# A record sort on one core: the rank picked out by TensorE and ScalarE in place of a product on VectorE, and three stages issued one unit further ahead

## The chip, the core and the metric

The kernel runs on one core of a Trainium2 chip. The metric is the time of one execution on the device in microseconds; lower is better. It is measured over several runs, and one more execution was profiled. The engines are named TensorE (PE, weight loads PEld), VectorE (DVE), ScalarE (ACT), GpSimd (POOL) and SyncE (SP). Each runs its own list of instructions in order and waits on semaphores for the others.

## The reference

Four layers of a graph network over 6250 nodes with 128 features and 200000 edges; each layer's result is added to its input and normalised. Only the edges matter here: every layer sums messages over the edges of a node.

```python
agg = jax.ops.segment_sum(msg, dst, num_segments=n_nodes)          # layer 0, mean over relations' messages
agg = jax.ops.segment_sum(val_exp[:, :, None] * h_neigh[edge_col], edge_row, num_segments=n)   # layer 1, attention
msg = jnp.where((edge_types == 0)[:, None], m_data, m_ctrl)        # layer 2
agg = jax.ops.segment_sum(msg, dst, num_segments=X.shape[0])
messages = norm[:, None] * h[col]                                  # layer 3
x = _layernorm(x + layer(x, edges))                                # four times
```

`src` and `dst` are data, so the kernel first sorts the edges on the chip into blocks by the tile of their target and the tile of their source. The four layers then work on those blocks.

## The kernel before, in words

About the first quarter of the span is the sort; the layers behind it need its whole result. An edge is a record of small bf16 fields, and 128 partitions times 1568 columns hold all of them. The sort has three levels, each of which distributes records by one digit of at most 14 values. The work is cut into **226 units**: 49 of level 1 (32 columns of records each, 14 digit values: tiles 448 wide), and then, in an order of groups of seven, 91 of level 2 and 86 of level 3 (28 columns each: tiles 392 wide). Forty-nine units of level 3 have a further place for records that overflow a bucket (`u.extra`; 16 digit places, tiles 448 wide), and seven units of level 2 are 112 wide. The units form two phases, level 1 and the rest, and the second begins when the last unit of the first is evicted.

A unit n passes through these steps, in lists written out by hand for each engine:

1. ScalarE, `double`: the unit's fields are copied in pairs into `V`, a ring of three (L429, L433, L437).
2. VectorE, `hot`: `O`, a one-hot of each record's digit, from `V` (L677).
3. TensorE, `count`: `pR` receives, for every record and every digit value, the number of records with this digit in front of it. One matmul with a triangle over the partitions (`tri_b`, L574) and 7 or 13 with ones (`ones_b`, L577) add into one PSUM bank of two.
4. ScalarE, `looked`: `R`, a bf16 copy of `pR` (L446).
5. VectorE: `M` = `O` times `R` (L730), which keeps only the count at the record's own digit; then `ranks`, a sum over the digits: `rank` (L687). A unit with an extra bucket adds three small instructions that change `O` and `rank` (L697, L699, L700).
6. ScalarE, `paired`: `place`, the rank in pairs (L455).
7. VectorE: `VO`, the fields times the one-hot (L740), and `PM`, a one-hot of the place in 128 columns (L91).
8. TensorE, `route`: 28 or 32 matmuls of `PM` and `VO` into `pV` (L593). ScalarE, `evict`: into `terms`, `second` or `recs` (L464, L470, L483).

VectorE's list for unit n is M(n), hot(n+1), ranks(n), VO(n), PM(n). TensorE's is count(n+1), route(n). ScalarE's is paired(n), evict(n-1), looked(n+1), in 147 units a copy for a small projection that TensorE makes in between (`xT` L539, `B` L544), then double(n+2), and in some units larger copies. In twelve units VectorE also unpacks sorted words (`words`, L712 and L714) between VO and PM.

The functions the diff touches:

Of the kernel before, what the change touches and what calls it, by code (L numbers as in the profile page):

```python
# [33 lines left out]
DIG, DIG_SHIFT, DIG_RECIP = 14, 16, 4682  # L34
# [4 lines left out]
def gnn_four_layers_kernel(nc, t, out):  # L39
# [30 lines left out]
    with ExitStack() as ctx:  # L70
        def sb(name, shape, dt, c=ctx):
            return c.enter_context(nc.sbuf_tensor(name, shape, dt))
# [84 lines left out]
        with ExitStack() as c1:  # L157
# [11 lines left out]
            zero_b = sb("zero_b", [P, P], BF16, c1)  # L169
# [4 lines left out]
            O = sb("O", [P, 2, 512], BF16, c1)  # L174
            R = sb("R", [P, 2, 512], BF16, c1)
            M = sb("M", [P, 512], BF16, c1)
# [25 lines left out]
                     "s_dup", "s_hot", "s_cnt", "s_look", "s_mul", "s_rank", "s_more", "s_pair", "s_val", "s_perm", "s_out", "s_ev",  # L202
                     "s_tp0", "s_xt0", "s_y0", "s_own0", "s_high0", "s_rest0", "s_mid0", "s_low0", "s_wt0", "s_total", "s_words", "s_named", "s_kind", "s_left", "s_last")
            (loads, pads, consts, tri_made, prep, fields, blanks, packed, s_pad, s_load, s_xin, s_stored, turned, wt_made,
             s_dup, s_hot, s_cnt, s_look, s_mul, s_rank, s_more, s_pair, s_val, s_perm, s_out, s_ev,
# [26 lines left out]
            done_with = {u.d: n + 1 for n, u in enumerate(units) if u.level == 3}  # L232
            SPLIT_AT, LIN_AT = A_N + 2, A_N + 28
            assert LIN_AT + 3 * NT <= UN
            PREP, FIELDS, PACKED = 15, 9, 6
            PADDED = 96

# [55 lines left out]
            with nc.Block() as block:  # L293
# [33 lines left out]
                def _(gp):  # L327
# [13 lines left out]
                    gp.memset(zero_b[:, :], 0.0).then_inc(consts, 1)  # L341
# [26 lines left out]
                    gp.wait_ge(consts, 11)  # L368
# [22 lines left out]
                def _(act):  # L391
# [47 lines left out]
                    def looked(n):  # L439

                        u = units[n]
                        k = u.npos * u.ngrp * u.w
                        act.wait_ge(s_cnt, n + 1)
                        if n >= 2:
                            act.wait_ge(s_mul, n - 1)
                        act.activation(R[:, n % 2, 0:k], pR[n % 2][:, 0:k], ACT.Copy).then_inc(s_look, 1)  # L446

                    def paired(n):

                        u = units[n]  # L450
                        cols = u.npos * u.ngrp
                        act.wait_ge(s_rank, n + 1)
# [71 lines left out]
                    for a, b in phases:  # L524
                        double(a)
                        double(a + 1)
                        looked(a)
                        for n in range(a, b):
                            paired(n)
                            if n > a:  # L530
                                evict(n - 1)
                            if n + 1 < b:
                                looked(n + 1)
                            i, sub = slot_of(n)
                            if sub == 1:
                                act.wait_ge(s_tp, i + 1)
                                if i >= 1:
                                    act.wait_ge(s_y, i)
                                act.activation(xT[:, :], pL[:, 0, :], ACT.Copy).then_inc(s_xt, 1)  # L539
                            if sub == 2:  # L540
                                act.wait_ge(s_y, i + 1)
                                if i % G7 == 0:
                                    act.wait_ge(s_rest, i // G7 + 1)
                                act.activation(B[:, i, :], pL[:, 1, :], ACT.Copy).then_inc(s_own, 1)  # L544
                            if n + 2 < b:
                                double(n + 2)
                            if n == A_N - 8:
                                weights_turned()
                            m, when = divmod(n - SPLIT_AT, 2)
                            if 1 <= m <= NB and when == 0:  # L550
                                mid_part(m - 1)
                            if 0 <= m < NB and when == 0:
                                high_part(m)
                            for d in range(LATE):
                                if n == done_with[d] + 3:
                                    places_and_high(d)
                                if n == done_with[d] + 6:
                                    sources_and_middle(d)
                        evict(b - 1)
# [4 lines left out]
                def _(pe):  # L564

                    def count(n):

                        u = units[n]
                        row = u.ngrp * u.w
                        k = u.npos * row  # L570
                        pe.wait_ge(s_hot, n + 1)
                        if n >= 2:
                            pe.wait_ge(s_look, n - 1)
                        pe.matmul(pR[n % 2][:, 0:k], tri_b[:, :], O[:, n % 2, 0:k], start=True, stop=False, skip_group_check=True)  # L574
                        for j in range(u.npos - 1):
                            m = u.npos - 1 - j
                            mm = pe.matmul(pR[n % 2][:, (j + 1) * row:k].rearrange("p (m r) -> p m r", r=row), ones_b[:, :],  # L577
                                           O[:, n % 2, j * row:(j + 1) * row].unsqueeze(1).broadcast_to([P, m, row]), start=False, stop=m == 1, skip_group_check=True)
                        mm.then_inc(s_cnt, 1)
# [17 lines left out]
                    pe.wait_ge(consts, 11)  # L597
# [32 lines left out]
                def _(v):  # L630
# [36 lines left out]
                    v.wait_ge(consts, 11)  # L667

                    def hot(n):

                        u = units[n]
                        cols = u.npos * u.ngrp
                        v.wait_ge(s_dup, n + 1)
                        if n >= 2:
                            v.wait_ge(s_val, n - 1)
                        o = O[:, n % 2, 0:cols * u.w].rearrange("p (n a b) -> p n a b", b=2, a=u.w // 2)
                        v.tensor_tensor(o, iota_1[:, 0:u.w].rearrange("p (a b) -> p a b", b=2).unsqueeze(1).broadcast_to([P, cols, u.w // 2, 2]),  # L677
                                        fields_of(n)[:, u.nf, :, :].unsqueeze(2).broadcast_to([P, cols, u.w // 2, 2]), ALU.is_equal).then_inc(s_hot, 1)

                    def ranks(n):  # L680
# [3 lines left out]
                        v.wait_ge(s_mul, n + 1)  # L684
                        if n >= 2:
                            v.wait_ge(s_pair, n - 1)
                        ins = v.tensor_reduce(rank[:, n % 2, 0:cols], M[:, 0:cols * u.w].rearrange("p (n a) -> p n a", a=u.w), AX.X, ALU.add)  # L687
                        if u.extra is None:
                            ins.then_inc(s_rank, 1)
                            return  # L690
                        ins.then_inc(s_more, 1)
                        mores[0] += 2
                        g, b = u.extra[1:]
                        o = O[:, n % 2, 0:cols * u.w].rearrange("p (a g w) -> p a g w", g=2, w=u.w)[:, :, g, :]
                        r = rank[:, n % 2, 0:cols].rearrange("p (a g) -> p a g", g=2)[:, :, g]
                        v.wait_ge(s_more, mores[0] - 1)
                        v.scalar_tensor_tensor(out=o[:, :, DIG], in0=r, scalar=float(P), in1=o[:, :, b], op0=ALU.is_ge, op1=ALU.mult).then_inc(s_more, 1)  # L697
                        v.wait_ge(s_more, mores[0])
                        v.scalar_tensor_tensor(out=r, in0=o[:, :, DIG], scalar=-float(P), in1=r, op0=ALU.mult, op1=ALU.add).then_inc(s_rank, 1)  # L699
                        v.tensor_tensor(o[:, :, b], o[:, :, b], o[:, :, DIG], ALU.subtract).then_inc(s_more, 1)  # L700
                        mores[0] += 1
# [19 lines left out]
                    mores = [0]  # L721
                    for a, b in phases:
                        hot(a)
                        for n in range(a, b):
                            u = units[n]
                            cols = u.npos * u.ngrp
                            v.wait_ge(s_look, n + 1)
                            if n >= 1:
                                v.wait_ge(s_rank, n)
                            v.tensor_tensor(M[:, 0:cols * u.w], O[:, n % 2, 0:cols * u.w], R[:, n % 2, 0:cols * u.w], ALU.mult).then_inc(s_mul, 1)  # L730
                            if n + 1 < b:
                                hot(n + 1)
                            ranks(n)
                            if n >= 2:
                                v.wait_ge(s_out, n - 1)
                            if u.extra is not None:
                                v.wait_ge(s_more, mores[0])
                            pairs = fields_of(n)[:, 0:u.nf, :, :]
                            where = O[:, n % 2, 0:cols * u.w].rearrange("p (n a b) -> p n a b", b=2, a=u.w // 2)
# [1743 lines left out]
```

## Time and profile before

| | us |
|---|---|
| median of 3 runs (lowest, highest) | 4307.43 (4306.51, 4310.26) |
| profiled execution, its own time | 4305.91 |
| its span, from the first to the last instruction | 4304.2 |
| VectorE busy in the span | 3648.7 (85%) |
| TensorE busy in the span | 3657.9 (85%) |
| ScalarE busy in the span | 2047.2 (48%) |
| GpSimd busy in the span | 431.4 (10%) |
| mean granted TensorE clock, as a share of 2.4 GHz | 0.945 |

The shares are means over all stages of the program, so they say little about the sort, which is the only stage that the diff touches. What bounds it is read from its own stretch, from the first O at 60.19 us to the last words at about 1135 us.

### The profile page before, as it was taken

To read this page: it belongs to the slowest core of one execution; us is meant where nothing else is said; L and a number is where in the kernel's file an instruction comes from. 1 tells how busy PE (TensorE), PEld (TensorE's weight loads), DVE (VectorE), ACT (ScalarE), POOL (GpSimd) and SP (SyncE) were. 2 spreads that over 40 slices of the span, in tenths; PEclk is the share of its full clock that TensorE was granted. 3 is DMA by queue.
4 is the path that set the end of the run, shared out by engine and by line. 5 is a ranking of instruction groups with operands and counts; after the bars stand their busy time and mean duration, and the time that the engine had idled before them with its cause. 6 is when DMAs were issued, how large, how long until landed. Compare 5 with 4: busy or idle time off the path is not lost. (4 is left out here: it accounts for less than half of the span.)

```text
span 4304.2 us, 94469 instructions
## 1 busy us (share of the span) xinstructions
PE 3657.9 (85%) x38991; PEld 3057.2 (71%) x38992; DVE 3648.7 (85%) x4714; ACT 2047.2 (48%) x4002; POOL 431.4 (10%) x335
## 2 busy tenths in 40 slices
PE   2665666666599999968999999997999999989998
PEld 2554555555466666648999999996888888867776
DVE  7999999999877777768999999998666666778897
ACT  2333333333355555532333333333666666757776
POOL 3002221230111111110000000001000000000000
PEclk9778899998799999978999999998999999989999
DMA  3000000000032222210000000001333333300000
GB/s 103 1 1 1 2 2 1 2 2 2 31 117 108 108 108 108 108 58 2 2 2 2 2 2 2 2 2 39 101 103 102 101 100 101 97 1 10 5 10 10
DMA packets 104807, 178.63 MB, mean 42 GB/s; under 512 B 11690, under 2 KB 101559, under 8 KB 104244
## 3 DMA queue, kind: packets, MB, share of 16 engines
q1 hardware_dynamic: 103892, 170.07, 12.1%
q8 instruction: 317, 5.19, 0.5%
q10 hardware_dynamic: 480, 2.40, 0.2%
q14 instruction: 118, 0.97, 0.1%
HBM read 86.93 MB, written 85.49 MB: 40 GB/s over the span
## 5 line engine op out<-in xcount | busy, mean ns | idle before, releaser
L97 DVE TENSOR_TENSOR both_hot<-iota_own,recs 128x1792 bf16<-128x1792 bf16 (+1 forms) x686 | 756.5, 1106 | 252.4 <-PE rR L1437 143.1
L1801 ACT ACTIVATE gC<-qC 128x896 f32<-128x896 f32 x343 | 314.6, 917 | 647.3 <-PE qC L1821 647.3
L1833 PE MATMUL qO<-A,gC 128*128 128x132 f32 x4802 | 615.2, 280 | 0.0
L593 PE MATMUL pV<-VO,PM 128*128 128x70 bf16 (+4 forms) x6524 | 295.3, 210 | 326.1 <-issue 322.7
L1833 PEld LDWEIGHTS qO<-A,gC 128*128 128x128 f32 x4802 | 566.4, 190 | 0.0
L593 PEld LDWEIGHTS pV<-VO,PM 128*128 128x128 bf16 x6524 | 272.3, 107 | 350.2 <-issue 348.8
L1445 PE MATMUL rO<-sl_f,terms 128*128 128x512 bf16 (+1 forms) x2058 | 500.1, 354 | 4.1 <-ACT sl_f L1403 2.5
L91 DVE TENSOR_TENSOR PM<-iota_b,place 128x3584 bf16<-128x3584 bf16 (+1 forms) x226 | 480.5, 2126 | 0.8 <-ACT place L455 0.8
L2145 ACT ACTIVATE some_r<-rC 128x512 fp32r<-128x512 f32 (+1 forms) x686 | 336.1, 543 | 253.0 <-PE rC L2175 252.6
L1403 ACT ACTIVATE sl_f<-rC 128x896 bf16<-128x896 f32 x343 | 314.0, 916 | 279.9 <-PE rC L1425 279.7
L91 DVE TENSOR_TENSOR places_hot<-iota_own,recs 128x896 bf16<-128x896 bf16 x700 | 403.2, 620 | 51.8 <-PE tC L2414 21.4
L1437 PE MATMUL rR<-rel_hot,both_hot 128*128 128x65 bf16 x2450 | 409.1, 193 | 0.0
L2396 ACT ACTIVATE tables_r<-tC 128x896 fp32r<-128x896 f32 x350 | 321.0, 919 | 143.5 <-PE tC L2414 142.8
L2426 PE MATMUL tO<-tables_r,Xr 128*128 128x448 f32 x1400 | 371.4, 387 | 9.1 <-ACT tables_r L2396 4.8
L1639 DVE TENSOR_TENSOR g<-sl_f 128x2688 bf16<-128x2688 bf16 (+1 forms) x229 | 363.5, 1587 | 0.2 <-PE qC L1821 0.2
L2187 PE MATMUL rK<-some_r,Xr 128*128 128x512 f32 (+1 forms) x1372 | 363.1, 386 | 0.0
L1821 PE MATMUL qC<-g,sl_f 128*128 128x128 bf16 x4908 | 313.5, 220 | 48.8 <-DVE g L1639 48.6
L2187 PE MATMUL rA<-all_r,Xr 128*128 128x512 f32 (+1 forms) x1372 | 342.1, 371 | 1.9 <-DVE all_r L1946 1.9
L1821 PEld LDWEIGHTS qC<-g,sl_f 128*128 128x128 bf16 x4908 | 292.1, 98 | 58.0 <-DVE g L1639 54.5
L577 PE MATMUL pR<-O,ones_b 128*128 128x392 bf16 (+16 forms) x2644 | 326.5, 281 | 0.0
L1445 PEld LDWEIGHTS rO<-sl_f,terms 128*128 128x128 bf16 x2058 | 201.0, 98 | 174.8 <-ACT sl_f L1403 5.9
L577 PEld LDWEIGHTS pR<-O,ones_b 128*128 128x128 bf16 x2644 | 255.7, 110 | 94.2 <-issue 30.2
(296 smaller groups left out, 6083.9 us busy)
## 6 DMA issues: line engine op xcount, KB each, us to landing
tables<-sl_f SPq DMA_DIRECT2D x343, 224.0 KB, 1.9
sl_f<-tables SPq DMA_DIRECT2D x343, 224.0 KB, 2.5
edges<-terms SPq DMA_DIRECT2D x1, 3528.0 KB, 11.2
B<-in_x SPq DMA_DIRECT2D x1, 2744.0 KB
out<-B SPq DMA_DIRECT2D x7, 392.0 KB
terms<-in_edge_type ACTq DMA_DIRECT2D x2, 686.0 KB
terms<-in_edge_weight ACTq DMA_DIRECT2D x1, 686.0 KB
recs<-in_src SPq DMA_DIRECT2D x1, 686.0 KB
```

Source lines behind the costliest of these rows:

```text
L91: return v.tensor_tensor(o.rearrange("p n (a b) -> p n a b", b=2), (iota_own if own else iota_b)[:, at:at + w].rearrange("p (a b) -> p a b ...
L97: return v.tensor_tensor(o.rearrange("p n k (a b) -> p (n k) a b", b=2), iota_own[:, 0:w].rearrange("p (a b) -> p a b", b=2).unsqueeze(1). ...
L577: mm = pe.matmul(pR[n % 2][:, (j + 1) * row:k].rearrange("p (m r) -> p m r", r=row), ones_b[:, :], O[:, n % 2, j * row:(j + 1) * row].unsq ...
L593: mm = pe.matmul(pV[n % 2][:, g * row:(g + 1) * row].rearrange("p (f b) -> p f b", f=u.nf), PM[:, n % 2, col, :], values[:, :, col, :], st ...
L1437: return pe.matmul(pR[:, to:to + DW], both_hot[:, U % 3, j, 0, :], rel_hot[:, K % 2, a % FOUR * n + j, 0:DW], start=a == 0 and j == 0, sto ...
L1445: mm = pe.matmul(pO[:, h, 0:(hi - lo) * P], X[:, a, s, :], of_half(kept[U % RING], h), start=a == 0 and s == 0, stop=a == NT - 1 and s == ...
L1639: v.tensor_tensor(h1[:, U % 2, 0:n, :, :].rearrange("p n s (a b) -> p n s a b", b=2), bare[U % 3][:, 0:n, 1, :].rearrange("p n (a b) -> p ...
L1821: mm = pe.matmul(pC[U % 2][:, tile_in_group(q, j), :], bare[U % 3][:, j, 0, :], h1[:, U % 2, j, s, :], start=s == 0 and (q > 0 or j != 1), ...
L1833: mm = pe.matmul(pO[i % SUMS][:, 0:XW], Cs[:, U % 2, j, :], A[:, a, :], start=a == 0, stop=a == NT - 1)
L2145: act.activation(of_half(some_r[:, U % 2, :], h).rearrange("p (n d) -> p n d", d=P), pC[Q % 3][:, 0:hi - lo, :], ACT.Copy).then_inc(s_cs, 1)
L2187: mm = pe.matmul((pA if whole else pK)[:, h, 0:(hi - lo) * P], Xr[:, a, s * P:(s + 1) * P], of_half((all_r if whole else some_r)[:, U % 2, ...
L2426: mm = pe.matmul(pO[:, h, 0:HW], Xr[:, max(b - 1, 0), s * P:(s + 1) * P], table_h[:, h, :], start=b == 0 and s == 0, stop=b == NX - 1 and ...
```

## The change

The product M on VectorE goes. A constant `lift` (2048 on the diagonal) is made on GpSimd at the start, and a further matmul with it in `count` adds 2048 to `pR` at each record's own digit. ScalarE's eviction becomes a Relu with a bias of -2048 per partition (`drop`), so that it writes `M` itself: the count at the own digit, zero elsewhere. `R` is gone; `M` has two buffers, `O` three. The one-hot, the counts and the evictions are issued two units ahead where they were one, and the doubled fields three ahead where they were two. A semaphore `s_taken` (rank read) takes the place of `s_mul` and `s_rank`.

```diff
-            zero_b = sb("zero_b", [P, P], BF16, c1)
+            lift = sb("lift", [P, P], BF16, c1)
+            drop = sb("drop", [P, 1], F32, c1)
...
-            O = sb("O", [P, 2, 512], BF16, c1)
-            R = sb("R", [P, 2, 512], BF16, c1)
-            M = sb("M", [P, 512], BF16, c1)
+            O = sb("O", [P, 3, 512], BF16, c1)
+            M = sb("M", [P, 2, 512], BF16, c1)
...
+                    gp.tensor_scalar(lift[:, :], ident_f[:, :], LIFT, None, ALU.mult).then_inc(consts, 1)
-                    gp.wait_ge(consts, 11)
+                    gp.wait_ge(consts, 12)
...
-                            act.wait_ge(s_mul, n - 1)
-                        act.activation(R[:, n % 2, 0:k], pR[n % 2][:, 0:k], ACT.Copy).then_inc(s_look, 1)
+                            act.wait_ge(s_taken, n - 1)
+                        act.activation(M[:, n % 2, 0:k], pR[n % 2][:, 0:k], ACT.Relu, bias=drop[:, 0:1]).then_inc(s_look, 1)
...
                         double(a)
                         double(a + 1)
+                        double(a + 2)
                         looked(a)
+                        looked(a + 1)
                         for n in range(a, b):
                             paired(n)
                             if n > a:
                                 evict(n - 1)
-                            if n + 1 < b:
-                                looked(n + 1)
...
-                                double(n + 2)
+                                looked(n + 2)
...
+                        pe.matmul(pR[n % 2][:, 0:k], lift[:, :], O[:, n % 3, 0:k], start=False, stop=False, skip_group_check=True)
...
                         count(a)
+                        count(a + 1)
                         for n in range(a, b):
-                            if n + 1 < b:
-                                count(n + 1)
+                            if n + 2 < b:
+                                count(n + 2)
...
                         hot(a)
+                        hot(a + 1)
                         for n in range(a, b):
...
-                            v.wait_ge(s_look, n + 1)
-                            if n >= 1:
-                                v.wait_ge(s_rank, n)
-                            v.tensor_tensor(M[:, 0:cols * u.w], O[:, n % 2, 0:cols * u.w], R[:, n % 2, 0:cols * u.w], ALU.mult).then_inc(s_mul, 1)
-                            if n + 1 < b:
-                                hot(n + 1)
                             ranks(n)
+                            if n + 2 < b:
+                                hot(n + 2)
```

(`double(n + 3)` stands just ahead of `looked(n + 2)`, behind the copies of the projection.)

VectorE's list in a unit with an extra bucket, level 3, before:

```order
L730 TENSOR_TENSOR M<-O,R 128x448
L677 TENSOR_TENSOR O<-iota,V 128x392
L687 TENSOR_REDUCE rank<-M 128x28
L697 SCALAR_TENSOR_TENSOR O<-rank,O 128x14
L699 SCALAR_TENSOR_TENSOR rank<-O,rank 128x14
L700 TENSOR_TENSOR O<-O 128x14
L740 TENSOR_TENSOR VO<-O,V 128x1792
L91 TENSOR_TENSOR PM<-iota_b,place 128x3584
```

The same place on VectorE in the changed program:

```order
L698 TENSOR_REDUCE rank<-M 128x28
L705 SCALAR_TENSOR_TENSOR O<-rank,O 128x14
L707 SCALAR_TENSOR_TENSOR rank<-O,rank 128x14
L708 TENSOR_TENSOR O<-O 128x14
L688 TENSOR_TENSOR O<-iota,V 128x448
L743 TENSOR_TENSOR VO<-O,V 128x1792
L91 TENSOR_TENSOR PM<-iota_b,place 128x3584
```

M is gone, and the one-hot O, now of the unit after next, stands between the last of the small instructions and VO.

ScalarE's list around one copy of the projection (xT), before; M and R are of the unit whose counts are ready, place is of the unit in work:

```order
L483 ACTIVATE recs<-pV 128x14x4 x2
L483 ACTIVATE recs<-pV 128x4
L446 ACTIVATE R<-pR 128x448
L539 ACTIVATE xT<-pL 128x128
L437 ACTIVATE V<-second 128x280
L455 ACTIVATE place<-rank 128x56
```

The same place on ScalarE in the changed program:

```order
L490 ACTIVATE recs<-pV 128x14x4 x2
L490 ACTIVATE recs<-pV 128x4
L546 ACTIVATE xT<-pL 128x128
L437 ACTIVATE V<-terms 128x336
L450 ACTIVATE M<-pR,drop 128x392
L462 ACTIVATE place<-rank 128x56
```

The eviction of the counts moved behind xT and V, so it is now the last thing ahead of the next unit's place.

## Rows read from the trace of the kernel before

**Rows 1.** Stretches: us; busy (instructions) of PE, PEld, DVE, ACT, POOL; clock; DMA.

```profile
66.00:304.00 238.00, 150.28 (x1953) 121.75 (x1954) 232.84 (x241) 82.40 (x197) 0.00 (x0) 0.80 0.07 19
304.00:312.00 8.00, 5.68 (x53) 4.54 (x52) 6.12 (x9) 1.87 (x5) 0.00 (x0) 0.50 0.00 1
312.00:1130.00 818.00, 537.84 (x7695) 436.37 (x7693) 782.79 (x1080) 302.36 (x1116) 179.29 (x113) 0.88 0.01 2
```

**Rows 2.** Waits of VectorE in the sort: us in total, times, longest us.

```profile
DVE M L730 <- ACT R L446: 28.3, 34, 3.3
DVE O L677 <- ACT V L433: 4.8, 8, 3.6
DVE PM L91 <- ACT place L455: 0.8, 1, 0.8
```

**Rows 3.** Timeline, level 1, VectorE: start us, duration us, instruction.

```profile
106.68 0.38 DVE L730 TENSOR_TENSOR M<-O,R 128x448 bf16<-128x448 bf16 x1
106.98 0.38 DVE L677 TENSOR_TENSOR O<-iota,V 128x448 bf16<-128x448 bf16 x1
```

**Rows 4.** Timeline, a plain unit of level 3, VectorE.

```profile
606.95 2.02 DVE L91 TENSOR_TENSOR PM<-iota_b,place 128x3584 bf16<-128x3584 bf16 x1
608.89 0.35 DVE L730 TENSOR_TENSOR M<-O,R 128x392 bf16<-128x392 bf16 x1
609.16 0.35 DVE L677 TENSOR_TENSOR O<-iota,V 128x392 bf16<-128x392 bf16 x1
609.43 0.55 DVE L687 TENSOR_REDUCE rank<-M 128x28 f32<-128x392 bf16 x1
609.90 0.96 DVE L740 TENSOR_TENSOR VO<-O,V 128x1568 bf16<-128x1568 bf16 x1
610.79 2.02 DVE L91 TENSOR_TENSOR PM<-iota_b,place 128x3584 bf16<-128x3584 bf16 x1
```

**Rows 5.** Timeline, end of a unit with an extra bucket, VectorE.

```profile
605.54 0.17 DVE L699 SCALAR_TENSOR_TENSOR rank<-O,rank 128x14 f32<-128x14 bf16 x1
605.63 0.21 DVE L700 TENSOR_TENSOR O<-O 128x14 bf16<-128x14 bf16 x1
605.95 1.09 DVE L740 TENSOR_TENSOR VO<-O,V 128x1792 bf16<-128x1792 bf16 x1
```

**Rows 6.** Groups: busy us, mean ns of one; idle before, releaser.

```profile
L730 DVE TENSOR_TENSOR M<-O,R 128x448 bf16<-128x448 bf16 (+2 forms) x226 | 87.0, 385 | 28.3 <-ACT R L446 28.3
L446 ACT ACTIVATE R<-pR 128x448 bf16<-128x448 f32 (+2 forms) x226 | 115.2, 510 | 220.9 <-PE pR L577 220.4
L455 ACT ACTIVATE place<-rank 128x56 bf16<-128x56 f32 (+1 forms) x226 | 57.8, 256 | 408.7 <-DVE rank L687 313.9 <-DVE rank L699 94.6
L355 POOL TENSOR_SCALAR terms<-terms 128x1568 int32<-128x1568 int32 x1 | 4.8, 4777 | 0.1
```

**Rows 7.** Timeline, TensorE, one route and one count at two times.

```profile
310.20 1.79 PE L593 MATMUL pV<-VO,PM 128*128 128x70 bf16 x28 [0.91 <-issue]
311.80 0.52 PE L574 MATMUL pR<-O,tri_b 128*128 128x392 bf16 x1
312.12 2.33 PE L577 MATMUL pR<-O,ones_b 128*128 128x364 bf16 x13
...
609.07 1.38 PE L593 MATMUL pV<-VO,PM 128*128 128x64 bf16 x28 [2.69 <-issue]
614.62 0.93 PE L593 MATMUL pV<-VO,PM 128*128 128x56 bf16 x28
615.39 0.33 PE L574 MATMUL pR<-O,tri_b 128*128 128x392 bf16 x1
615.55 1.27 PE L577 MATMUL pR<-O,ones_b 128*128 128x364 bf16 x13
```

**Rows 8.** Timeline, VectorE, the starts of both phases.

```profile
63.18 0.39 DVE L730 TENSOR_TENSOR M<-O,R 128x448 bf16<-128x448 bf16 x1 [2.60 <-ACT R L446]
...
305.82 0.36 DVE L730 TENSOR_TENSOR M<-O,R 128x392 bf16<-128x392 bf16 x1 [3.26 <-ACT R L446]
```

More of the change, by code:

```diff
@@ L232, in gnn_four_layers_kernel @@
             done_with = {u.d: n + 1 for n, u in enumerate(units) if u.level == 3}
+            mores_of = {n: 3 * i for i, n in enumerate(n for n, u in enumerate(units) if u.extra is not None)}
             SPLIT_AT, LIN_AT = A_N + 2, A_N + 28
@@ L236, in gnn_four_layers_kernel @@
             PADDED = 96
+            LIFT = 2048.0
+            assert 8 * P < LIFT and DIG * P < LIFT
             LATE = ND1 - 2
@@ L340, in _ @@
                     gp.memset(ones_b[:, :], 1.0).then_inc(consts, 1)
-                    gp.memset(zero_b[:, :], 0.0).then_inc(consts, 1)
+                    gp.memset(drop[:, :], -LIFT).then_inc(consts, 1)
                     gp.memset(ident_f[:, :], 0.0).then_inc(tri_made, 1)
@@ L451, in paired @@
                         cols = u.npos * u.ngrp
-                        act.wait_ge(s_rank, n + 1)
+                        if u.extra is None:
+                            act.wait_ge(s_taken, n + 1)
+                        else:
+                            act.wait_ge(s_more, mores_of[n] + 2)
                         if n >= 2:
@@ L544, in _ @@
                                 act.activation(B[:, i, :], pL[:, 1, :], ACT.Copy).then_inc(s_own, 1)
+                            if n + 3 < b:
+                                double(n + 3)
                             if n + 2 < b:
-                                double(n + 2)
+                                looked(n + 2)
                             if n == A_N - 8:
@@ L573, in count @@
                             pe.wait_ge(s_look, n - 1)
-                        pe.matmul(pR[n % 2][:, 0:k], tri_b[:, :], O[:, n % 2, 0:k], start=True, stop=False, skip_group_check=True)
+                        pe.matmul(pR[n % 2][:, 0:k], tri_b[:, :], O[:, n % 3, 0:k], start=True, stop=False, skip_group_check=True)
+                        pe.matmul(pR[n % 2][:, 0:k], lift[:, :], O[:, n % 3, 0:k], start=False, stop=False, skip_group_check=True)
                         for j in range(u.npos - 1):
@@ L577, in count @@
                             mm = pe.matmul(pR[n % 2][:, (j + 1) * row:k].rearrange("p (m r) -> p m r", r=row), ones_b[:, :],
-                                           O[:, n % 2, j * row:(j + 1) * row].unsqueeze(1).broadcast_to([P, m, row]), start=False, stop=m == 1, skip_group_check=True)
+                                           O[:, n % 3, j * row:(j + 1) * row].unsqueeze(1).broadcast_to([P, m, row]), start=False, stop=m == 1, skip_group_check=True)
                         mm.then_inc(s_cnt, 1)
@@ L666, in _ @@
                     v.wait_ge(prep, PREP)
-                    v.wait_ge(consts, 11)
+                    v.wait_ge(consts, 12)
                     def hot(n):
@@ L736, in _ @@
                             if u.extra is not None:
-                                v.wait_ge(s_more, mores[0])
+                                v.wait_ge(s_more, mores_of[n] + 3)
                             pairs = fields_of(n)[:, 0:u.nf, :, :]
-                            where = O[:, n % 2, 0:cols * u.w].rearrange("p (n a b) -> p n a b", b=2, a=u.w // 2)
+                            where = O[:, n % 3, 0:cols * u.w].rearrange("p (n a b) -> p n a b", b=2, a=u.w // 2)
                             v.tensor_tensor(VO[:, n % 2, 0:cols * u.nf * u.w].rearrange("p (f n a b) -> p f n a b", b=2, a=u.w // 2, f=u.nf),
```

29 lines of the change are left out of this document (12 added, 17 removed).

## The prediction

> **What bounds the kernel now.** The busy shares of the whole span say nothing here, because the diff touches only the sort; so I read the stretches of the sort first. In level 1 VectorE is busy 232.84 of 238.00 us and in levels 2 and 3 782.79 of 818.00, that is 98% and 96%, while TensorE has 150.28 and 537.84 and ScalarE 82.40 and 302.36 [rows 1]. The reader is to see that VectorE has hardly a gap and every other engine many. The list of waits then tells what VectorE's gaps are: 28.3 us in 34 waits of the product M for the evicted counts R, and 4.8 us in 8 waits of the one-hot O for V [rows 2]. It hardly ever waits for `place` (0.8 us, once). Everything behind the sort needs its whole result, so a microsecond taken out of VectorE's list is a microsecond of the kernel, as long as the others keep up.
>
> **What goes: 226 products.** A neighbour starts before an instruction has ended, so the price of one is from its start to the next start, not its duration. A 448-wide M starts at 106.68 and the next O at 106.98: 0.30 us of a duration of 0.38 [rows 3]. A 392-wide one takes 608.89 to 609.16: 0.27 [rows 4]. By the loops there are 98 of 448 (49 of level 1, 49 with an extra bucket), 121 of 392 and 7 of 112, for which I take half of 0.27. That is 98 x 0.30 + 121 x 0.27 + 7 x 0.13 = **63.0 us**. The instruction behind PM is then the reduction, which waits for a look that was due a unit earlier.
>
> The Trainium skill ("VectorE: DVE Perf Modes", The DRAIN you can't avoid) says that the next operation does not start until the pipe is empty. By that, a product would give back its whole busy time, 87.0 us in the group of M [rows 6], 24 more than I count. The starts 0.30 us apart under a duration of 0.38 [rows 3] speak against it.
>
> **What goes: waits for the counts.** Two of the 34 waits are the starts of the phases, 2.60 and 3.26 us [rows 8], where nothing can lie ahead. The other 32 are 28.3 - 2.60 - 3.26 = **22.4 us**. They come where TensorE is slow: R(n+1) is behind route(n-1) and count(n+1), both of which start only after PM(n-1), and M(n+1) wants it one VectorE unit later. In the change the counts that come behind the same route are those of the unit after, wanted a whole unit later. Of the waits of O for V, the one at the phase start (3.6, the longest [rows 2]) stays; the other seven, 1.2 us, go, since V too is a unit ahead: **1 us**.
>
> **What goes: a bubble in 49 units.** In a unit with an extra bucket VO must wait for the last small write: from its start at 605.63 to VO at 605.95 it is 0.32 us, where the one ahead of it, which nobody waits for, takes 605.54 to 605.63, 0.09 [rows 5]. In the change the one-hot stands between, which reads nothing of it. I take 0.20 us of the 0.23: **10 us**, bounds 0 and 11.
>
> **What comes.** *TensorE:* one matmul of 392 or 448 columns per unit. The triangle of the same width takes 615.39 to 615.55, 0.16 us, at the high clock and 311.80 to 312.12, 0.32 us, at the low one [rows 7]. TensorE's work in a plain unit at the high clock becomes route 0.93 (to its modelled end) + count 615.39 to 616.82, 1.43, + 0.16 = 2.5 us against a VectorE unit of 608.89 to 610.79 plus the PM of 1.94 (606.95 to 608.89), less M: 1.90 + 1.94 - 0.27 = 3.57 us [rows 4, 7]. Hidden by 1 us; the projection (three matmuls and a transpose in turn over three units) fits into it.
>
> *ScalarE:* the same evictions, 0.51 us on average [rows 6], now with a bias read per partition; it is idle most of the sort, so only two of them, at the phase starts, are on the path. The Trainium skill ("ScalarE: Activation LUTs", What ACT_TABLE_LOAD costs) gives about 0.09 us for each such operand; by it two evictions on the path would cost 0.2 us, and no row here shows it apart. Relu is no table switch: both built programs have four table loads.
>
> *The cover that could go* is the order on ScalarE: `place` of unit n+1 now stands behind the eviction of the counts of unit n+2. Count from the start of unit n's reduction, which is the end of PM(n-1). PM(n+1) wants `place` after a whole unit, 3.57, and reduction, O and VO of the next, 0.47 + 0.27 + 0.89 = 1.63: at 5.2 us. ScalarE's chain at the high clock is route 0.93, count 1.59, eviction 0.5 + 0.1 (a guess for the bias), place 0.26 [rows 6], and some 0.2 for handing over: 3.6 us, 1.6 early. At the low clock it is route 1.79, count 311.80 to 314.45, 2.65, + 0.32, then 0.6, 0.26, 0.2: 5.8 us, 0.6 late [rows 4, 7]. So a unit at the low clock can still cost 0.6 us, and if it does not, nothing is lost. The stretch of levels 2 and 3 had a granted clock of 0.88, which is 24% of it at 1.2 GHz, and the slow route at 609.07 came after 2.69 us of idle TensorE [rows 1, 7]. Shorter VectorE units and one more matmul shorten that idle time; long gaps stay in the twelve units with `words` and at the phase starts. I take **3 us** (some five stalls of 0.6); bounds 0 and 32 x 0.6 = 19.
>
> *Start of the sort:* GpSimd makes `lift` as the last constant, and VectorE and TensorE wait for it. The nearest row is a tensor_scalar of 1568 columns in 4.78 us [rows 6]; for 128 that is 0.4, with a fixed part 0.5. The longer first count (0.4) and the missing M and O on the chain cancel: **0.5 us**.
>
> *Start of the second phase*, at the low clock (0.50 in that stretch [rows 1]): ScalarE now evicts the second unit's counts ahead of the first `place`, and a slow count of 2.97 us with an eviction of 0.6 lies there where reduction, O and VO fill only 1.63: 1.9 late, less the one-hot that is already done, 0.27, and a little for the longer VO of level 2: **1.5 us**, bounds 0.3 and 3.
>
> **Sum.** 63.0 + 22.4 + 1 + 10 - 3 - 0.5 - 1.5 = 91.4 us off the profiled execution's 4305.9 (span 4304.2 and 1.7 around it): 4214.5. The median of the runs shown lies 1.5 above that execution, so I say **4216 us**.
>
> **Rivals.**
> *The waits come back as waits for `place`.* For it: the chain above is late by 0.6 in a slow unit, and the 32 old waits averaged 0.7 us. Against it: TensorE has less idle time, and 1.6 us of slack at the high clock. Then the 22.4 us are not gained: 4216 + 22 - 3 = 4235; 0.18.
> *TensorE becomes the bound and the kernel slower.* If the granted clock stayed at 1.2 GHz, a unit would take TensorE 1.79 + 2.65 + 0.32 = 4.8 us and the projection some 0.5 more per unit, 5.3 against VectorE's 4.2 on average with its words and small instructions ((818 - 81) / 177). Each slow unit then costs 1.1 us; 91 us are eaten at 83 slow units in a row of 177, about half; with all of them slow it is +195 - 91, 4410. Against it: 24% were slow when TensorE had more idle time [rows 1]. 0.04.
> *The product is worth its whole busy time.* 87.0 instead of 63.0: 4192; 0.03. The skill's page quoted above is its reason, the starts in rows 3 and 4 are against it.
> *The change does not do what it says*, because VectorE meets the same length of chain elsewhere: waits for `place` of 0.4 us in each of 226 units would take all of it, and the slack of 1.6 us must be wrong by 2. 0.03, time 4307.
>
> **Numbers.** My forecast (4207 to 4226) has 0.72. With the returning waits in part or whole, to 4240, it is 0.72 + 0.15; the lower end is the sum with no stalls and the full bubble, about 4210, less some microseconds for the phases behind the sort: 4205. Range **4205 to 4240**. What a measurement of this kernel can tell from no change is about 0.2%, 8.6 us. Faster: 0.72 + 0.18 + 0.03 = 0.93; same 0.03; slower 0.04.
>
> **What would show it.** Right: VectorE's list has four large instructions per unit, 3.57 us in plain units and 0.30 less than before in level 1; the waits of a reduction for the look are two, at the phase starts; the sort ends about 91 us earlier and every stage behind it is as long as before; the granted clock in the sort rises. The bubble is right if O follows the last small instruction within 0.15 us. Wrong: waits of PM for `place` of more than 10 us, a granted clock under 0.88 in levels 2 and 3, reductions that wait for M in mid-phase, or routes that start later than PM's end in many units.

## The result and the profile after

| | before | changed |
|---|---|---|
| median | 4308.85 us (4 runs, 4306.51 to 4313.77) | 4203.91 us (4 runs, 4203.23 to 4205.06) |
| profiled execution, its span | 4305.9, 4304.2 us | 4203.2, 4201.5 us |
| granted clock over the span | 0.945 | 0.958 |

The ratio is 0.9765 (95% interval 0.9754 to 0.9777; the quotient of the two medians is 0.9756): 104.9 us less by the medians, 102.7 between the profiled executions. The forecast was 4216, 91.4 less; the time lies 1.1 us under the low end of its range. The direction was right, the mechanism too, and one term was too small.

First the page of the changed kernel, its first lines:

```profile
span 4201.5 us, 94346 instructions
...
PE 3645.2 (87%) x39093; PEld 3045.7 (72%) x39218; DVE 3569.6 (85%) x4488; ACT 2086.5 (50%) x4002; POOL 451.9 (11%) x336
```

Next, stretches: us; busy (instructions) of PE, PEld, DVE, ACT, POOL; granted clock; DMA share, GB/s. They are cut at the first one-hot of level 1, at that of level 2, where VectorE's last `words` start, and at the end. Of the kernel before, by the same cut (other than that of [rows 1]):

```profile
60.19:302.20 242.01, 152.60 (x1963) 123.08 (x1963) 235.69 (x245) 83.03 (x199) 0.00 (x0) 0.80 0.10 28
302.20:1134.40 832.20, 546.36 (x7779) 443.00 (x7779) 791.73 (x1091) 305.05 (x1124) 179.29 (x113) 0.87 0.01 2
1134.40:4304.20 3169.80, 2958.98 (x29249) 2491.10 (x29249) 2583.05 (x3331) 1643.17 (x2668) 214.67 (x195) 0.97 0.16 52
```

And of the changed kernel:

```profile
60.17:287.17 227.00, 154.03 (x2012) 120.33 (x2012) 220.67 (x197) 87.92 (x198) 0.00 (x0) 0.84 0.10 29
287.17:1025.80 738.63, 537.71 (x7956) 431.86 (x7956) 724.82 (x914) 338.95 (x1124) 196.48 (x113) 0.93 0.01 2
1025.80:4201.50 3175.70, 2953.50 (x29125) 2493.52 (x29249) 2584.61 (x3331) 1643.20 (x2668) 215.57 (x195) 0.97 0.16 52
```

Level 1 is 15.0 us shorter, levels 2 and 3 are 93.6 shorter, and what follows is 5.9 longer: 15.0 + 93.6 - 5.9 = 102.7. The forecast had 14.7 in level 1 (49 products of 0.30), a loss of 0.5 ahead of the first one-hot, 91.4 - 14.7 + 0.5 = 77.2 in levels 2 and 3, and none behind. So 16.4 us are to be explained in levels 2 and 3, and 5.9 behind the sort. Below, "the sort" is the first two stretches, 1074.2 and 965.6 us.

The timeline of VectorE in level 1, changed kernel (start, duration, instruction):

```profile
189.63 0.61 DVE L698 TENSOR_REDUCE rank<-M 128x32 f32<-128x448 bf16 x1
190.16 0.37 DVE L688 TENSOR_TENSOR O<-iota,V 128x448 bf16<-128x448 bf16 x1
190.46 1.54 DVE L743 TENSOR_TENSOR VO<-O,V 128x2688 bf16<-128x2688 bf16 x1
191.92 2.28 DVE L91 TENSOR_TENSOR PM<-iota_b,place 128x4096 bf16<-128x4096 bf16 x1
194.13 0.60 DVE L698 TENSOR_REDUCE rank<-M 128x32 f32<-128x448 bf16 x1
```

Four instructions per unit, 194.13 - 189.63 = 4.50 us. Before it was 4.80, the product's 0.30 more: behind the product at 106.68 in [rows 3] the next one starts at

```profile
111.48 0.38 DVE L730 TENSOR_TENSOR M<-O,R 128x448 bf16<-128x448 bf16 x1
```

The end of a unit with an extra bucket, which answers to [rows 5]:

```profile
597.27 0.18 DVE L707 SCALAR_TENSOR_TENSOR rank<-O,rank 128x14 f32<-128x14 bf16 x1
597.36 0.21 DVE L708 TENSOR_TENSOR O<-O 128x14 bf16<-128x14 bf16 x1
597.45 0.39 DVE L688 TENSOR_TENSOR O<-iota,V 128x448 bf16<-128x448 bf16 x1
597.75 1.08 DVE L743 TENSOR_TENSOR VO<-O,V 128x1792 bf16<-128x1792 bf16 x1
```

The last small write is now followed after 0.09 us instead of 0.32, and VO follows the one-hot after its usual 0.30. The waits of VectorE in the sort (us in total, times, longest), answering to [rows 2]:

```profile
DVE rank L698 <- ACT M L450: 6.1, 2, 3.3
DVE PM L91 <- ACT place L462: 4.6, 8, 0.9
DVE O L688 <- ACT V L437: 3.6, 1, 3.6
```

Where 34 waits for counts stood, two are left, the phase starts; the rest of the old waits has not come back as waits for `place`. Of the groups (busy us, mean ns; idle before), two:

```profile
L450 ACT ACTIVATE M<-pR,drop 128x448 bf16<-128x448 f32 (+2 forms) x226 | 135.0, 597 | 111.1 <-PE pR L587 109.1 <-DVE rank L698 1.9
L584 PE MATMUL pR<-O,lift 128*128 128x448 bf16 (+2 forms) x226 | 85.6, 379 | 0.0
```

The eviction costs 597 ns against 510 [rows 6], and the new matmul stands in line with no idle time before it.

### The profile page after: what moved, and what is told of

Its sections match the earlier page's. It is cut to its first block and busy times, and to the rows that moved or that the text cites. A ratio compares the mean times of both kernels' runs of the same rounds, so it can differ in the third digit from the quotient of the medians.

```text
span 4201.5 us, 94346 instructions
## 1 busy us (share of the span) xinstructions
PE 3645.2 (87%) x39093; PEld 3045.7 (72%) x39218; DVE 3569.6 (85%) x4488; ACT 2086.5 (50%) x4002; POOL 451.9 (11%) x336
## 5 line engine op out<-in xcount | busy, mean ns | idle before, releaser
L603 PE MATMUL pV<-VO,PM 128*128 128x70 bf16 (+4 forms) x6524 | 268.4, 202 | 248.4 <-issue 242.4
L1448 PE MATMUL rO<-sl_f,terms 128*128 128x384 bf16 (+1 forms) x1934 | 471.2, 352 | 3.3 <-ACT sl_f L1406 2.5
L603 PEld LDWEIGHTS pV<-VO,PM 128*128 128x128 bf16 x6524 | 246.0, 102 | 274.2 <-issue 273.7
L587 PEld LDWEIGHTS pR<-O,ones_b 128*128 128x128 bf16 x2644 | 242.7, 105 | 98.9 <-issue 24.5
L587 PE MATMUL pR<-O,ones_b 128*128 128x392 bf16 (+16 forms) x2644 | 299.7, 267 | 0.0
```

The source lines that it names most:

```text
L603: mm = pe.matmul(pV[n % 2][:, g * row:(g + 1) * row].rearrange("p (f b) -> p f b", f=u.nf), PM[:, n % 2, col, :], values[:, :, col, :], st ...
L1448: mm = pe.matmul(pO[:, h, 0:(hi - lo) * P], X[:, a, s, :], of_half(kept[U % RING], h), start=a == 0 and s == 0, stop=a == NT - 1 and s == ...
```

## The experiments

Every row of this table is one kernel's profiled execution: stretches cut as above, and the median of its runs (of e3 and e4 one run each). The ratio is to runs of the kernel before taken beside it, whose medians are 4308.85 for the changed kernel and 4305.66 to 4306.65 for the others.

| kernel | level 1 | levels 2, 3 | sort | median (ratio to before, 95%) |
|---|---|---|---|---|
| before | 242.0 | 832.2 | 1074.2 | 4308.85 |
| changed | 227.0 | 738.6 | 965.6 | 4203.91 (0.9754 to 0.9777) |
| e1 look-ahead alone | 241.5 | 804.9 | 1046.4 | 4281.77 (0.9926 to 0.9959) |
| e2 lift alone | 233.7 | 766.9 | 1000.6 | 4241.83 (0.9829 to 0.9862) |
| e3 before, GpSimd's sort work cut | 241.9 | 802.9 | 1044.8 | 4300.41 |
| e4 changed, GpSimd's sort work cut | 227.0 | 709.3 | 936.2 | 4194.01 |
| e5 changed, one-hot behind VO | 227.0 | 767.0 | 994.0 | 4229.42 (0.9802 to 0.9832) |
| e6 changed, lift matmul twice | 227.4 | 742.2 | 969.6 | 4209.67 (0.9765 to 0.9795) |
| e7 changed, x copies ahead of the fields | 227.0 | 738.6 | 965.6 | 4201.29 (0.9742 to 0.9769) |
| e8 before, counts evicted behind V | 241.8 | 831.3 | 1073.1 | 4305.22 (0.9987 to 1.0005) |
| e9 changed, once more | 227.0 | 738.9 | 965.9 | 4205.32 (0.9745 to 0.9775) |

**e1: the look-ahead without the lift.** The kernel before with a third buffer of O and one-hots, counts and fields a unit further ahead; the product and R stay.

```diff
-            O = sb("O", [P, 2, 512], BF16, c1)
+            O = sb("O", [P, 3, 512], BF16, c1)
...
+                            if n + 3 < b:
+                                double(n + 3)
                             if n + 2 < b:
-                                double(n + 2)
+                                looked(n + 2)
...
-                            if n + 1 < b:
-                                count(n + 1)
+                            if n + 2 < b:
+                                count(n + 2)
...
-                            if n + 1 < b:
-                                hot(n + 1)
+                            if n + 2 < b:
+                                hot(n + 2)
                             ranks(n)
```

> The kernel before with the look-ahead alone: the product M stays on VectorE, the one-hots, counts, evictions and fields go one unit further ahead. My theory: the 22.4 us of waits for R in mid-phase and the 1.2 us of O for V go, the bubble in the 49 units with an extra bucket stays, and VectorE instructions lengthened by GpSimd fall by at most 10 us: 4274 to 4286 us. Rival (the chain of route, count and eviction comes back as waits for place): 4300 to 4309 us.

Measured 4281.77, in the expected range, sort 27.8 us shorter, nearly all of it (27.3) in levels 2 and 3. VectorE's waits from level 2 on:

```profile
DVE O L680 <- ACT V L433: 4.5, 3, 3.6
DVE PM L91 <- ACT place L455: 3.8, 5, 1.5
DVE M L734 <- ACT R L446: 2.9, 1, 2.9
```

The waits for counts are gone but for the phase start, and 3.8 us of waits for `place` have come. That the look-ahead removes these waits is shown. It gives 27.3 us net, and the forecast's terms for it come to 22.4 + 1 - 3 - 1.5 = 18.9.

**e2: the lift without the look-ahead.** The changed kernel with the order of before.

```diff
-                            if n + 3 < b:
-                                double(n + 3)
                             if n + 2 < b:
-                                looked(n + 2)
+                                double(n + 2)
...
-                            if n + 2 < b:
-                                count(n + 2)
+                            if n + 1 < b:
+                                count(n + 1)
...
                             ranks(n)
-                            if n + 2 < b:
-                                hot(n + 2)
+                            if n + 1 < b:
+                                hot(n + 1)
```

> The changed kernel with the look-ahead of the kernel before: the product is gone, one-hots, counts and evictions are one unit ahead, fields two. My theory: 63 us of products and 11 us of bubbles go, but the reduction now wants the evicted counts 0.3 us earlier than the product did, at the low clock about 1.9 us late, so the waits of VectorE for the eviction rise from 28 us to between 35 and 75: 4235 to 4275 us. Rival (the look-ahead buys nothing once the product is gone): 4200 to 4215 us.

Measured 4241.83, in the expected range, sort 73.6 us shorter. The waits for counts are now the reduction's (whole sort):

```profile
DVE rank L695 <- ACT M L450: 31.7, 37, 3.8
```

They had been expected to rise to between 35 and 75 us; they stayed near the 28.3 of before.

In levels 2 and 3 the two parts give 27.3 and 65.2 us, 92.5 together, of 93.6 measured for both: they add. In level 1 they do not: 0.5 + 8.4 of 15.0. Without look-ahead a level-1 unit that has lost its product is short enough to wait for its counts, which the unit of before was not: 24 of the 37 waits, 24.5 us, lie in levels 2 and 3, and the other 13, 7.3 us, in level 1, where the changed kernel has one, at the phase start.

**e3 and e4: is it GpSimd?** My first theory for the missing microseconds was that GpSimd's work in the sort stretches VectorE's instructions, less so in the changed order. Both kernels had GpSimd's elementwise steps cut to four columns.

```diff
-                        gp.tensor_tensor(xrest[:, :, :], B[:, T, :], X[:, T, 0, :], ALU.subtract).then_inc(s_rest, 1)
+                        gp.tensor_tensor(xrest[:, 0:1, 0:4], B[:, T, 0:4], X[:, T, 0, 0:4], ALU.subtract).then_inc(s_rest, 1)
```

(and the same for the other steps of the weights, the kinds and the low parts of x). What is left out VectorE clears behind the sort, where the two kernels take 3194.7 and 3196.2 us, so their medians say nothing of the sort; the stretches do.

> The kernel before with GpSimd's work inside the sort cut to four columns per instruction, which leaves out the low parts of x, the relation codes and the weights' rests (VectorE clears their places after the sort). My theory: the 35 us by which VectorE's starts in levels 2 and 3 are late beyond the waits named in the trace are GpSimd's doing, so the stretch from the first O to the last words falls from 1074 to about 1040 us. Rival (they are not GpSimd's): it stays above 1065 us.

> The changed kernel with the same cut of GpSimd's work in the sort. My theory: the same lateness is 20 us here, so the stretch from the first O to the last words falls from 966 to about 946 us, and the gap between the two kernels' stretches shrinks from 109 to about 94 us, which is near the forecast of 91. Rival (the missing 15 us have nothing to do with GpSimd): the gap stays at 105 to 111 us.

Levels 2 and 3 of the two kernels, columns as above:

```profile
301.13:1104.00 802.87, 540.42 (x7779) 438.74 (x7779) 758.47 (x1091) 305.38 (x1124) 81.40 (x69) 0.88 0.01 2
...
286.83:996.10 709.27, 521.74 (x7956) 422.22 (x7956) 696.72 (x913) 341.63 (x1124) 90.16 (x69) 0.96 0.01 2
```

As a reason for the missing microseconds the theory fell, though e3 came near its 1040 us. GpSimd's busy time falls from 179.29 to 81.40 us and from 196.48 to 90.16, and both sorts get 29.4 us shorter, so the gap between them stays 108.5. GpSimd costs VectorE much, but the same in both.

With GpSimd nearly out of the way the rest can be counted. I took each start-to-start distance of two neighbouring instructions of VectorE in levels 2 and 3, less the median for that pair, and call the sum the lateness (the starts of the phases left out). In e3 it is 27.9 us of M behind R (the list shows 28.4 - 3.3 = 25.1 of idle), **8.2 us of O behind V**, and 0.8 of PM behind `place`, 36.9 in all; in e4 it is 3.9, all for `place`. That is 33 us where the forecast had 18.9. (On the kernel before itself, where GpSimd's steps blur the count, M is late by 25.2.) The 8.2 is what I had missed: the list names 12 waits of O for V, 5.6 us, of which 3.6 is the phase start, so 2.0 of the 8.2. Most of the rest is in 30 one-hots that start late, 0.17 us on average, with no wait named: about half of that is idle time of under 0.15 us, which the list leaves out, and the end of the instruction ahead covers the other half. On the kernel before, one such place:

```profile
603.29 0.54 ACT L446 ACTIVATE R<-pR 128x448 bf16<-128x448 f32 x1 [1.94 <-PE pR L577]
603.73 0.27 ACT L544 ACTIVATE B<-pL 128x128 f32<-128x128 f32 x1
603.87 0.39 DVE L730 TENSOR_TENSOR M<-O,R 128x448 bf16<-128x448 bf16 x1 [0.83 <-ACT R L446]
603.89 0.44 ACT L437 ACTIVATE V<-second 128x280 bf16<-128x280 bf16 x1
604.36 0.36 DVE L677 TENSOR_TENSOR O<-iota,V 128x392 bf16<-128x392 bf16 x1
```

M waits for R. V stands behind R and a copy on ScalarE and ends at 604.33; O starts at 604.36, 0.49 after M instead of 0.30, and its row names no wait.

**e8: is O's lateness a cost of its own?** If V's place behind R were all, evicting the counts behind V would give it back on the kernel before.

```diff
                             if n > a:
                                 evict(n - 1)
-                            if n + 1 < b:
-                                looked(n + 1)
...
                             if n + 2 < b:
                                 double(n + 2)
+                            if n + 1 < b:
+                                looked(n + 1)
```

> The kernel before with one move on ScalarE: the eviction of the counts goes behind the projection's copies and the doubled fields, so V no longer stands behind R. The two runs without GpSimd's work put the 15 us that the forecast missed on VectorE's starts that were late without a wait named: O came 0.1 to 0.2 us late behind V in some 40 units, 8 us in all, where the list of waits showed 1.2. My new theory: this lateness of O goes, the late M stay, 4296 to 4302 us, the stretch from the first O to the last words 6 to 10 us shorter than 1074. Rival (O is late for another reason, or R comes later by as much): 4303 to 4309 us, the stretch above 1071.

Measured 4305.22, a ratio of 0.9987 to 1.0005: no change. Waits of VectorE in the sort:

```profile
DVE M L730 <- ACT R L446: 34.0, 42, 3.3
...
DVE O L677 <- ACT V L433: 3.6, 1, 3.6
```

O's waits are gone but for the phase start, and M's rose from 28.3 to 34.0: R is later by what V is earlier. The rival held. R and V, behind the count, are one chain on ScalarE, and a move within it gains nothing; the 23.4 us that I put down were the part of its cost that the list shows. Look-ahead takes VectorE off the chain (e1). It is not the only thing that helps: in e2, with the product gone and the look-ahead of before, the waits of O for V in mid-phase are down to one of 0.2 us.

**e5: the one-hot behind VO.** The changed kernel with O(n+2) moved, to see the bubble by itself.

```diff
                             ranks(n)
-                            if n + 2 < b:
-                                hot(n + 2)
...
                                             pairs.unsqueeze(3).broadcast_to([P, u.nf, cols, u.w // 2, 2]), ALU.mult).then_inc(s_val, 1)
+                            if n + 2 < b:
+                                hot(n + 2)
```

> The changed kernel with the one-hot of unit n+2 behind VO(n) where it stood between the small instructions and VO(n). My theory: VO again waits for the last small write in the 49 units with an extra bucket, 0.23 us each, 11 us more: 4213 to 4218 us. Rival (the gap before VO has another reason, or the place of the one-hot does not matter): 4202 to 4207 us.

Measured 4229.42, sort 28.4 us longer than the changed kernel's. One unit with an extra bucket, and the first row of the list of waits:

```profile
605.97 0.21 DVE L708 TENSOR_TENSOR O<-O 128x14 bf16<-128x14 bf16 x1
606.29 1.09 DVE L741 TENSOR_TENSOR VO<-O,V 128x1792 bf16<-128x1792 bf16 x1
607.30 0.86 DVE L688 TENSOR_TENSOR O<-iota,V 128x392 bf16<-128x392 bf16 x1
608.08 2.01 DVE L91 TENSOR_TENSOR PM<-iota_b,place 128x3584 bf16<-128x3584 bf16 x1
...
DVE PM L91 <- ACT place L462: 22.5, 26, 3.2
```

The bubble is back (605.97 to 606.29; 0.31 is the median), 49 x 0.22 = 10.8 us, as expected of it. But the total missed the expected range: waits for `place` went from 4.6 to 22.5 us in 26 places, and 10.8 + 17.9 is 28.7 of the 28.4. The one-hot is what TensorE's count waits for: counted from the end of PM(n-1), the median count of n+2 starts after 1.89 us where it was 1.02, and its eviction, ahead of the next `place`, ends after 4.43 where it was 3.47. So the place of O ahead of VO is worth two things, and the second, the larger, was in no sum of mine.

**e6: the lift matmul twice.** The changed kernel with half the weight, issued two times per unit.

```diff
+                        pe.matmul(pR[n % 2][:, 0:k], lift[:, :], O[:, n % 3, 0:k], start=False, stop=False, skip_group_check=True)
```

> The changed kernel with the lift made in two matmuls of 1024 each, so 226 more matmuls of 392 or 448 columns, 0.16 to 0.19 us each at the high clock, 36 to 43 us of TensorE in all. My theory: TensorE's idle time covers it, 4202 to 4207 us. Rival (TensorE and ScalarE's chain is already the bound in a part of the units): 4212 us or more, with waits of PM for place above 10 us.

Measured 4209.67, 5.8 us over the changed kernel, between the theory's range and the rival's, with runs from 4205.8 to 4216.1; the sort of its profile is 4.0 longer, waits for `place` 6.1 us instead of 4.6. At 0.16 us each, the price at the high clock, 226 more matmuls are 36 us of TensorE, so VectorE's work covers most of a second one, not all. TensorE is not the bound.

**e7: the copies of x ahead of the fields.** Five of the eight waits for `place` lie where ScalarE has the larger copies; on the changed kernel, behind a slow count:

```profile
309.16 2.33 PE L587 MATMUL pR<-O,ones_b 128*128 128x364 bf16 x13
...
312.01 0.94 ACT L527 ACTIVATE terms<-xrest 128x896 bf16<-128x896 f32 x1
312.86 0.94 ACT L521 ACTIVATE terms<-B 128x896 bf16<-128x896 f32 x1
313.70 0.23 ACT L462 ACTIVATE place<-rank 128x56 bf16<-128x56 f32 x1
313.96 3.00 DVE L91 TENSOR_TENSOR PM<-iota_b,place 128x3584 bf16<-128x3584 bf16 x1 [0.63 <-ACT place L462]
```

```diff
-                            if n + 3 < b:
-                                double(n + 3)
-                            if n + 2 < b:
-                                looked(n + 2)
                             if n == A_N - 8:
                                 weights_turned()
...
                                     sources_and_middle(d)
+                            if n + 3 < b:
+                                double(n + 3)
+                            if n + 2 < b:
+                                looked(n + 2)
```

> The changed kernel with ScalarE's larger copies (high and middle parts, words' places and sources) ahead of double and the eviction of the counts, no longer between that eviction and the next place. My theory: of the 4.6 us in 8 waits of PM for place some 3 to 4 go, 4199 to 4202 us. Rival (the copies then delay the counts' eviction as much as they delayed place): 4203 to 4206 us.

The waits for `place` fall to 1.4 us, those of O for V rise from 3.6 to 5.5, and the sort is the same, 965.6. In the sort the rival held: ScalarE is as late at another instruction. The median, 4201.29, is in the theory's range and 2.6 under the changed kernel's, but with overlapping ratios, and its profile has that outside the sort, where the theory had no gain; it is no proof of a better version.

**e9: the changed kernel again.**

> The changed kernel once more, next to the run above on the same chip, to see how much the stretch behind the sort differs from run to run. My theory: the stretch from the first O to the last words is 966 again within 2 us, and what is behind it differs from 3176 by up to 4 us, so the 2.6 us of the version with ScalarE's copies moved forward are nothing that the move did: 4201 to 4206 us. Rival (the move gained 2.6 us): 4204 us or above with a stretch behind the sort of 3175 to 3177.

Measured 4205.32, sort 965.9 and 3175.2 behind it, both as in the changed kernel's first profile. It does not settle e7: a median above 4204 with 3175 to 3177 behind the sort is also what the rival named for a gain by e7's move. Whether that move gains anything stays open.

## Why the prediction was right in direction and too small

- **Products, 63.0 us: right.** Level 1, which had no waits in mid-phase, shortened by 49 x 0.30 and a little. By the rule of the Trainium skill ("VectorE: DVE Perf Modes", The DRAIN you can't avoid) that the next operation waits for an empty pipe, weighed before as a rival, a unit there would have lost the whole 0.38; the trace has 4.80 to 4.50. The same section adds, and the prediction left out, that a next operation that is not held starts earlier; with this the trace agrees (0.30 us from start to start under 0.38).
- **Bubble, 10 us: right.** 0.32 became 0.09: 49 x 0.23 = 11.3, and e5 brings it back.
- **Waits, 22.4 + 1 us: the step that failed, by its size.** The mechanism (counts, and V, a unit further ahead) is what e1 shows. Counted in e3 and e4 it is worth 36.9 - 0.8 = 36 us of lateness, 33 net of what comes as waits for `place`, against 23.4 and 18.9. I took the waits from the list ("the other seven, 1.2 us, go"), and the list leaves out short idle times and what hides under the tail of the instruction ahead: about 0.08 us at each of some 35 products, and 8.2 us of one-hots behind V of which it names 2. 33 - 18.9 = 14, with 1.3 from the bubble, is 15.4 of the 16.4; the last 1 stays open. Nor is all of it the look-ahead's: e1 gave 27.3, and e2 65.2, where products (48.3) and bubbles (11.3) come to 59.6. The 5.6 more came with the lift alone.
- **Stalls for `place`, 3 us, and the phase start, 1.5: right as a sum.** The stalls are 4.6 us in eight waits, all where the low clock was forecast to cost something: over the 6 us ahead of each the granted clock was 0.50 to 0.72, so 1.2 GHz for more than half of the time, where the stretch has 0.93. But slow units are not enough: 18 more, with less than 0.75 over the same 6 us, had no wait. In five of the eight the larger copies of x stand ahead of `place`, which no term had; in e7, with these copies moved, three of the five still had 0.72 to 0.76 and no wait. The start of the second phase cost 0.1: its first PM came 6.02 us after its first O, 5.88 before, because the second count turned to the high clock midway (its matmuls of ones take 1.41 us at 290.99, 2.33 in the first).
- **Start of the sort, 0.5: not seen.** VectorE's wait for GpSimd's last constant rose from 6.8 to 7.5 us, but the first one-hot came at 60.17 us instead of 60.19, and in the other runs anywhere from 59.22 to 63.43.
- **Lift matmul: right.** Its 0.33 and 0.16 us stand in the rows below. In level 1 the granted clock made no difference: 227.0 us at 0.84 in the changed kernel and at 0.94 in e5. The granted clock in levels 2 and 3 rose from 0.87 to 0.93, and TensorE's busy time fell there from 546 to 538 us with 177 instructions more. The low clock, on which the rivals of returning waits and of TensorE as the bound rest, became rarer.
- **Behind the sort, "as long as before": wrong by 5.9 us** (3169.8 to 3175.7, 3175.2 in e9). e2 has 3175.1 too; e1, e5, e6, e7 and e8 have 3171.5 to 3172.8. Nothing there was edited, and no run isolates it. Each figure is of one execution, and nine executions of the kernel before, taken together, lie from 4302.36 to 4312.26, so it may be no effect of the change at all. The cause is open.

Timeline of the changed kernel at the start of the second phase, TensorE at the low and, 8 us later, the high clock:

```profile
287.58 0.51 PE L583 MATMUL pR<-O,tri_b 128*128 128x392 bf16 x1 [1.49 <-DVE O L688]
287.88 0.53 PE L584 MATMUL pR<-O,lift 128*128 128x392 bf16 x1
288.21 2.33 PE L587 MATMUL pR<-O,ones_b 128*128 128x364 bf16 x13
...
290.99 1.41 PE L587 MATMUL pR<-O,ones_b 128*128 128x364 bf16 x13
...
296.40 0.33 PE L584 MATMUL pR<-O,lift 128*128 128x392 bf16 x1
296.56 1.27 PE L587 MATMUL pR<-O,ones_b 128*128 128x364 bf16 x13
297.88 0.59 ACT L450 ACTIVATE M<-pR,drop 128x392 bf16<-128x392 f32 x1 [0.31 <-PE pR L587]
```

From the lift's start to the next it is 0.33 us, then 0.16.

## What to carry to other kernels

Price an instruction that goes by its start-to-start distance, and waits that go by the lateness of each instruction against the usual distance to its neighbour, not by the idle time in a list of waits: on an engine that is busy 96% of the time much of the lateness hides in gaps too short for the list and under the instruction ahead. Two late operands that one engine makes in turn are one chain; moving one of them ahead only delays the other (e8, e7), and with look-ahead by a whole unit and the product gone neither is left (e4). An instruction that feeds another engine's chain is worth its position as well as its time (e5: 28 us, the bubble among them, for a move of one that takes 0.35).

## What was not expected of the hardware

- **GpSimd holds VectorE.** Cutting 98 and 106 us of GpSimd's work shortened both sorts by 29.4 us, where no wait of VectorE in levels 2 and 3 names GpSimd. On the changed kernel:

```profile
303.21 5.04 POOL L379 TENSOR_TENSOR xrest<-B,terms 128x896 f32<-128x896 f32 x1 [243.25 <-ACT terms L521]
303.41 1.17 DVE L743 TENSOR_TENSOR VO<-O,V 128x1960 bf16<-128x1960 bf16 x1
304.50 2.02 DVE L91 TENSOR_TENSOR PM<-iota_b,place 128x3584 bf16<-128x3584 bf16 x1
...
306.43 0.55 DVE L698 TENSOR_REDUCE rank<-M 128x28 f32<-128x392 bf16 x1
306.90 1.57 DVE L688 TENSOR_TENSOR O<-iota,V 128x392 bf16<-128x392 bf16 x1
308.40 1.17 DVE L743 TENSOR_TENSOR VO<-O,V 128x1960 bf16<-128x1960 bf16 x1
```

  The one-hot takes 1.57 us instead of 0.35 and ends 0.2 us after GpSimd's step, at 308.47 and 308.25; the reduction ahead of it, which reads one tensor, has its usual 0.55. VO and PM, with two inputs, have their usual 1.17 and 2.02 in the same step, so not every such instruction is held. Over levels 2 and 3 of the changed kernel 44 instructions of VectorE last more than 0.1 us longer than the median of their kind, 26.8 us in all. Each has two inputs and overlaps a step of GpSimd, and none of the 45 reductions that overlap one is among them. The Trainium skill ("GPSIMD Engine Reference", Specifications) says that GpSimd's SBUF interfaces are shared with VectorE, with contention where VectorE's instruction runs in a 2-port perf mode or has two SBUF inputs; these counts agree.
- **The eviction with a bias read per partition takes 0.09 us more**: 0.50 to 0.59 for 392 columns, 0.54 to 0.63 for 448. It also became a Relu where it was a copy, and no run separates the two. The Trainium skill ("ScalarE: Activation LUTs", What ACT_TABLE_LOAD costs) has about 93 ns for each such operand, and the trace agrees.
- **TensorE's clock in level 1 went its own way.** It was 0.80 before and 0.84 in the changed kernel, but 0.93 with the lift matmul issued twice (e6) and 0.94 with the same matmuls as the changed kernel and a later one-hot (e5). With 49 matmuls more, TensorE's busy time there was 145.1 us in e6 against 154.0. What raised the clock no run isolates.
